# First experts' down product: the last 48 hidden channels in both partition halves, each half making 128 output channels in a bank of its own

## What is computed

```
h = silu(einsum('td,eid->eti', xt, W1)) * einsum('td,eid->eti', xt, W3)
expert_out = einsum('eti,edi->etd', h, W2)
y = einsum('etd,te->td', expert_out, combine)
z = silu(xt @ Ws1.T) * (xt @ Ws3.T) @ Ws2.T
```

## Time and profile before

| | us |
|---|---|
| median of 3 runs (1195.98 to 1196.88) | 1196.71 |
| the profiled execution | 1198.59 |
| span of its trace | 1196.8 |
| PE busy in the span | 1089.0 (91%) |
| DVE, ACT, POOL busy | 495.3, 503.4, 440.0 |

### The profile page before, as it was taken

How to read it: one execution, slowest core, us unless ns; L and a number is a source line. 1 busy time by engine, 2 the same in 40 slices (tenths; PEclk the granted TensorE clock), 3 DMA queues, 4 the chain that set the end, 5 groups by cost and what they waited for, 6 DMA issues and landing times. The chain is left out here.

```text
span 1196.8 us, 29018 instructions
## 1 busy us (share of the span) xinstructions
PE 1089.0 (91%) x10258; PEld 840.3 (70%) x10259; DVE 495.3 (41%) x1340; ACT 503.4 (42%) x1306; POOL 440.0 (37%) x563
## 2 busy tenths in 40 slices
PE   8889989988798689999988999998679999999998
PEld 4466666765465347777756777776579899899997
DVE  2365656555560013323325666766443800000423
ACT  2445554444432123333324666575334333333333
POOL 2122031311348852777644666332514100200434
PEclk9999999999998669999998999998789999999999
DMA  6199477120373334565546111000157655555673
GB/s 201 45 322 362 145 253 250 37 87 32 156 227 124 121 112 131 150 192 149 144 135 257 37 37 48 27 19 3 54 193 230 191 162 186 174 178 175 194 241 105
DMA packets 119340, 176.09 MB, mean 147 GB/s; under 512 B 17441, under 2 KB 96913, under 8 KB 117777
## 3 DMA queue, kind: packets, MB, share of 16 engines
q1 hardware_dynamic: 94992, 136.08, 35.4%
q0 software_dynamic: 9696, 26.75, 6.9%
q10 hardware_dynamic: 14544, 11.75, 3.0%
HBM read 105.07 MB, written 68.16 MB: 145 GB/s over the span
## 5 line engine op out<-in xcount | busy, mean ns | idle before, releaser
L3137 PE MATMUL bank<-w,m_HT 128*128 x624 | 141.0, 379 | 0.0
L2975 ACT ACTIVATE m_HT<-bank,m_b 128x128 f32<-128x128 f32 x312 | 88.8, 369 | 88.9 <-PE bank L3123 72.9
L3137 PEld LDWEIGHTS bank<-w,m_HT 128*128 128x128 f32 x624 | 115.7, 190 | 14.1
L1820 PE MATMUL bank<-m_W,m_XGT 128*128 x316 | 114.5, 487 | 10.8 <-issue 8.5
L1434 POOL DMA_INDIRECT GA<-ys,r_pos x64 | 64.7, 1010 | 64.7 <-DVE m_US L1764 46.5
L1677 ACT ACTIVATE m_XGT<-bank 128x256 f32<-128x256 f32 x79 | 30.3, 383 | 133.5 <-DVE m_US L1764 82.3
L1756 DVE TENSOR_TENSOR m_H<-bank,m_SG 128x176 f32<-128x176 f32 x79 | 26.9, 341 | 139.9 <-ACT m_SG L1681 108.0
L1820 PEld LDWEIGHTS bank<-m_W,m_XGT 128*128 128x128 f32 x316 | 57.0, 201 | 32.3 <-issue 16.4
L3123 PE MATMUL bank<-m_XGT,m_w1a 128*128 128x128 f32 x640 | 77.2, 279 | 2.3 <-issue 2.0
L2939 POOL DMA_INDIRECT m_GA<-ys,r_pos x32 | 31.4, 980 | 129.0 <-SPq L2890 120.0
L3123 PEld LDWEIGHTS bank<-m_XGT,m_w1a 128*128 128x128 f32 x640 | 75.0, 195 | 2.9 <-issue 2.3
(11 more groups left out here) (472 smaller groups left out, 2302.8 us busy)
## 6 DMA issues: line engine op xcount, KB each, us to landing
m_w1a<-in_m_w SPq DMA_DIRECT2D x20, 1024.0 KB
m_w<-in_m_w SPq DMA_DIRECT2D x19, 1024.0 KB
xs<-zeros SPq DMA_DIRECT2D x1, 10112.0 KB, 34.4
ys<-zeros SPq DMA_DIRECT2D x1, 10112.0 KB, 34.4
ys<-m_US ACTq DMA_DIRECT2D x79, 128.0 KB
m_GS<-xs SPq DMA_DIRECT2D x72, 128.0 KB
w<-in_m_w SPq DMA_DIRECT2D x8, 1024.0 KB, 10.6
xs<-zeros SPq DMA_DIRECT2D x1, 6400.0 KB, 23.4
```

The source lines that it names most:

```text
L1820: last = nc.tensor.matmul(BU[b % 2][:, 0:IW], XGT[:, b % 2, m * P:(m + 1) * P], W13[:, m, bass.ds(e, 1), :], start=m == 0, stop=m == KC - 1)
L2975: last = nc.scalar.activation(HT[:, b % 2, at, :], BU[i][:, c * P:(c + 1) * P], ACT.Gelu, bias=b1[:, b % WB, at:at + 1])
L3137: last = nc.tensor.matmul(BY[b % 2][:, 0:DIM], HT[:, b % 2, c, :], w2[:, bass.ds(e, 1), c, :], start=c == 0, stop=c == CH - 1)
```

## The change

The down product of a tile is cut into two halves of 128 output channels, and each half has a bank: `BY[0]` for the channels 0 to 127, `BY[1]` for 128 to 255, in every tile. The chunk of 128 hidden channels makes two matmuls of 128 columns (all 128 rows of the array). The rest of 48 is copied by ACT to partitions 0 to 47 and to 64 to 111 of `HT`. Then the first half's rest is multiplied from partitions 0 to 63 with `W2B`, and the second half's from partitions 64 to 127 with `odd[b]`: four buffers in the upper half of `W2B`, which SP fills per tile from DRAM (48 partitions of 512 bytes) with `load_odd`. Since both banks are used by every tile, the down product of tile j now waits until DVE has copied tile j - 1 out (`y_used`, counted one higher everywhere). DVE copies in two halves. Two small edits on POOL replace a semaphore by its step counter.

```diff
+        HALF = P // 2
+        odd = [W2B[HALF:P, b // 2, b % 2 * P:(b % 2 + 1) * P] for b in range(4)]
...
                     sp.dma_start(XG[:, b, :].unsqueeze(1), slots[:, bass.ds(s, 1), :]).then_inc(ld_x[b], 16)
+                    sp.wait_ge(ld_odd, 16 * j - 64)
+                    load_odd(j - 4, b)
+
+                def load_odd(j, b):
+                    e = sp.value_load(r.texp[0:1, bass.ds(j, 1)], min_val=0, max_val=E0 - 1)
+                    sp.dma_start(odd[b][0:KI].unsqueeze(1), io["w2"][P:I0, bass.ds(e, 1), P:DIM]).then_inc(ld_odd, 16)
...
+                sp.wait_ge(ld_w, 80)
+                for j in range(FIRST - 4):
+                    if j:
+                        sp.wait_ge(ld_odd, 16 * j)
+                    load_odd(j, j)
                 load(FIRST, FIRST % 4, FIRST)
...
+                for j in range(NT - 4, NT):
+                    sp.wait_ge(ld_odd, 16 * j)
+                    sp.wait_ge(y_full, j - 3)
+                    load_odd(j, j % 4)
...
                     nc.scalar.activation(HT[:, b % 2, 0, :], BH[b % 2][:, 0:P], ACT.Copy)
-                    nc.scalar.activation(HT[0:KI, b % 2, 1, :], BH[b % 2][0:KI, P:2 * P], ACT.Copy).then_inc(ht_used, 1)
+                    for lo in (0, HALF):
+                        last = nc.scalar.activation(HT[lo:lo + KI, b % 2, 1, :], BH[b % 2][0:KI, P:2 * P], ACT.Copy)
+                    last.then_inc(ht_used, 1)
...
-                    nc.vector.tensor_copy(Y[:, b % 2, :], BY[b % 2][:, 0:DIM]).then_inc(y_used, 1)
+                    for half in range(2):
+                        last = nc.vector.tensor_copy(Y[:, b % 2, half * P:(half + 1) * P], BY[half][:, 0:P])
+                    last.then_inc(y_used, 1)
...
-                    if not follows(ahead, 2):
-                        pe.wait_ge(y_used, j - 1)
+                    pe.wait_ge(y_used, j + 1)
                     pe.wait_ge(ht_used, j + 1)
-                    nc.tensor.matmul(BY[b % 2][:, 0:DIM], HT[:, b % 2, 0, :], W2A[:, bass.ds(e, 1), :],
-                                     start=True, stop=False)
-                    nc.tensor.matmul(BY[b % 2][:, 0:DIM], HT[:, b % 2, 1, :], W2B[:, bass.ds(e, 1), :],
-                                     start=False, stop=True).then_inc(y_full, 1)
+                    for half in range(2):
+                        nc.tensor.matmul(BY[half][:, 0:P], HT[:, b % 2, 0, :],
+                                         W2A[:, bass.ds(e, 1), half * P:(half + 1) * P], start=True, stop=False)
+                    pe.wait_ge(ld_odd, 16 * j + 16)
+                    nc.tensor.matmul(BY[0][:, 0:P], HT[0:HALF, b % 2, 1, :], W2B[0:HALF, bass.ds(e, 1), 0:P],
+                                     start=False, stop=True)
+                    nc.tensor.matmul(BY[1][:, 0:P], HT[HALF:P, b % 2, 1, :], odd[b], start=False, stop=True).then_inc(y_full, 1)
```

More of the change, by code:

```diff
@@ L1529, in moe0 @@
         z_full, z_used = sem("z_full"), sem("z_used")
-        sent, in_place, z_added = [sem(f"sent{b}") for b in range(2)], sem("in_place"), sem("z_added")
+        sent, in_place, ld_odd = [sem(f"sent{b}") for b in range(2)], sem("in_place"), sem("ld_odd")
+        HALF = P // 2
+        odd = [W2B[HALF:P, b // 2, b % 2 * P:(b % 2 + 1) * P] for b in range(4)]
         slots, rows_out = (x.rearrange("(s p) d -> p s d", p=P) for x in (fx.xs, fx.ys))
@@ L1609, in add_shared @@
                     pool.wait_ge(z_used, t // 2 + 1)
-                    nc.gpsimd.tensor_tensor(part, part, Z[:, t, half * P:(half + 1) * P], ALU.add).then_inc(z_added, 1)
+                    return nc.gpsimd.tensor_tensor(part, part, Z[:, t, half * P:(half + 1) * P], ALU.add)
                 for t in range(TILES):
@@ L1621, in _ @@
                 landed(TILES - 1)
+                own = fx.pool_steps
                 for half in range(2):
-                    add_shared(TILES - 1, half)
-                pool.wait_ge(z_added, 2 * TILES)
-                own = fx.pool_steps
+                    last = add_shared(TILES - 1, half)
+                own(pool, last)
                 def may_fetch(t):
-                    pool.wait_ge(y_used, pool.value_load(r.ready[0:1, t:t + 1], min_val=3, max_val=NT + 2))
+                    pool.wait_ge(y_used, pool.value_load(r.ready[0:1, t:t + 1], min_val=4, max_val=NT + 3))
                     pool.sem_inc(due, 1)
@@ L1685, in turned_product @@
                     nc.scalar.activation(HT[:, b % 2, 0, :], BH[b % 2][:, 0:P], ACT.Copy)
-                    nc.scalar.activation(HT[0:KI, b % 2, 1, :], BH[b % 2][0:KI, P:2 * P], ACT.Copy).then_inc(ht_used, 1)
+                    for lo in (0, HALF):
+                        last = nc.scalar.activation(HT[lo:lo + KI, b % 2, 1, :], BH[b % 2][0:KI, P:2 * P], ACT.Copy)
+                    last.then_inc(ht_used, 1)
                 def store(j, b):
                     s = act.value_load(r.tslot[0:1, bass.ds(j, 1)], min_val=0, max_val=NT - 1)
-                    act.wait_ge(y_used, j + 1)
+                    act.wait_ge(y_used, j + 2)
                     act.dma_start(rows_out[:, bass.ds(s, 1), :], Y[:, b % 2, :].unsqueeze(1)).then_inc(stored[b % 2], 16)
@@ L1749, in _ @@
                                ((POOL_GATES, POOL_GATES + 1), (POOL_GATES + 2,)))
-                r.ready_on_dve(nc, dve, fx.ident[:], BU[0], BU[1], 2, gated,
+                r.ready_on_dve(nc, dve, fx.ident[:], BU[0], BU[1], 3, gated,
                                ((POOL_GATES + 3,), (POOL_GATES + 4,)))
@@ L1763, in step @@
                     dve.wait_ge(stored[b % 2], 8 * (j + (2 - b % 2)))
-                    nc.vector.tensor_copy(Y[:, b % 2, :], BY[b % 2][:, 0:DIM]).then_inc(y_used, 1)
+                    for half in range(2):
+                        last = nc.vector.tensor_copy(Y[:, b % 2, half * P:(half + 1) * P], BY[half][:, 0:P])
+                    last.then_inc(y_used, 1)
+                dve.sem_inc(y_used, 1)
                 product(0, 0)
```

## The result

The kernel after takes 1232.72 us (median of 4, 1229.84 to 1233.63) where the kernel before takes 1196.8 (median of 4: the three executions of the table above and one of 1202.01): ratio 1.0281, 95% interval 1.0255 to 1.0307, 36 us slower. The span of its trace is 1230.4 us.

A forecast was written before the change was run, and what follows sets the result against it. PE was taken to bound the steady steps, late handovers the scatter stretch. PE's steps 10.1, SP's chain 3.3, scatter stretch 3.5 and tail 0.8 sum to 17.7 us over 1196.7: 1214 us, range 1204 to 1230.

The forecast's parts named there:

- Full-array part: Down product on PE, chunk of 128 hidden channels: four passes of 128 columns cost 0.448 us instead of 0.434, +0.014.
- paired part: Down product's rest of 48 on PE: row halves run side by side, 0.22 us instead of 0.434, plus changes of form.
- round trip: PE's way into the half-row form and out again around the down product: 0.33 to 0.34 us a step.
- SP's chain: SP's odd loads per tile: serial loop of landing, table read and issue, 2.63 us; +3.3 us after slack of 6.3.
- need rounds: SP, first 32 tiles: every fourth round has a third table read and the `in_place` wait, 0.87 us each, 7.0 us.
- SP sets the pace: Rival: landing takes 2.1 us or more and PE stops each step at `ld_odd`; 1222 to 1235 us, chance 0.20.
- Scatter stretch: 390 to 436 us, while POOL scatters: waiting for the previous tile's copy closes a loop, 10.6 us a step; +3.5 us.
- Tail: End of the tile loop: the last two down products both wait for two copies, +0.8 us.

The follow-up runs named there:

- before_half_rows: The kernel before with the last 48 channels' two passes on 64 array rows alone, same bank, nothing paired; 1167.81 us beside 1142.74, ratio 1.0229.
- two_in_flight: The kernel after with odd transfers alternating between two semaphores, so SP waits for the last landing but one; 1163.76 us, ratio 1.0169 to the kernel before.
- two_in_flight_early: The kernel after with two semaphores for odd transfers and the second layer's weights requested at about 320 us; 1159.84 us, ratio 1.0129 to the kernel before.
- before_cut: The kernel before with the down product's four passes of 256 columns cut into eight of 128, same bank; 1206.16 us beside 1194.27, ratio 1.0095.
- full_rows_two_banks_b: The kernel after without form change, odd transfers and ACT's second copy, last 48 channels over all 128 rows; fourth chip, 1217.41 us beside 1199.53, ratio 1.0156.
- after_again: The kernel after, unchanged, run on the second chip; 1172.85 us, ratio 1.0253 to the kernel before.

## Why the prediction was wrong in size

The direction, and most terms of the sum, held. One was several times too small, and it put the time outside the range of 1204 to 1230 us; a small one was missing.

- **Full-array part and paired part: right.** 0.142 us a step was forecast, 2.64 - 2.49 = 0.15 measured. The round trip of 0.34 us read from rows 4 and 5 is what before_half_rows shows by itself, and the halves pair.
- **SP's chain: the failed step.** "7.0 + 2.6 - 6.3 = +3.3 us" came out at 15.5 us on the second chip and 13.8 on the fourth (medians). By the distances from tile 10 to 75 it is 14.0 and 11.8 there, and on the first some 22.8 - 65 x 0.19 = 10.5. Two inputs were off. The landing was taken as 1.9 us throughout; idle it is 1.6, but in traffic up to 3.0, and waiting for one at a time costs 9.1 us (two_in_flight). And `weights()` was costed by the 2.9 us in which it holds the queue, not by the bytes in front of the next landing: 253 to 267 GB/s from 548 to 554 us, odd weights that PE could use 4.0 us after their issue instead of 1.9, and the granted clock of 0.50 behind the stop. The stop is 7.9 us in that trace, 2.6 were forecast; with two semaphores in place, taking it away gave 3.9 us more. SP's own rounds, which the sum charged with 7.0 us against a slack of 6.3, were not the trouble: the need rounds cost 1.0 each and not 0.87, and two_in_flight_early still loses nothing by them. The prediction saw the steepness ("+14 us more" from 2.15 us on) and put it into the rival *SP sets the pace*, 1222 to 1235 us, with a chance of 0.20. That rival's time came true; its shape did in part, since PE stopped for SP in single steps and once for long, and not in each.
- **Missing: the queue of PE.** The prediction counted passes by their duration alone. Shorter passes leave the queue less lead for its table reads; before_cut shows it, and the kernel after loses at most 0.04 us a step by it, 0.5 to 2.4 us in 65 steps. Also, `ld_odd` is waited for by register work of the queue (the order after shows `REGISTER_ALU [waits m0_ld_odd]`), so a late landing should also delay the table read behind it. I read this from the order and have not measured it alone.
- **Scatter stretch: the loop as forecast, its price not settled.** The loop was forecast at 10.6 us a step and ran at 10.9. From 390 to 436 us four down products begin, as forecast; before it were five, where the prediction read 5.8 steps from the number of passes. The price of +3.5 us, with 0.3 for the form in the two steps from tile 8 to 10, stands against 4.9 us on the first chip and 3.8 on the fourth. That full_rows_two_banks_b loses nothing while in the loop forbids calling this more than agreement of one or two traces; it may be luck.
- **Tail: small.** 0.8 forecast; the distance from tile 75 to 78 grows by 1.0 us, and the last product itself by 0.7.
- **Not in the sum: 3 us ahead of the first tile.** Tile 0 starts 3.0 us later on the first chip and 4.1 on the fourth, but 0.3 earlier on the second. By 334 us, before any edited instruction, PE of the two kernels already stands 2.9, 1.7 and -3.2 us apart. Most of it is thus variation between executions. Counted from POOL's first scatter, tile 0 comes 0.6, 0.9 and 0.9 us later in the kernel after; that part may be of the edits.

The sum of the distances on the first chip: 3.0 + 4.9 + 8.6 + 7.7 + 6.5 + 1.0, and 0.7 for the last product, is 32.4 of the 33.6 us between the spans.

## What to carry to other kernels

A transfer added to each step of a loop is a chain of its own. Cost it at the landing time in the traffic where it runs, keep more than one in flight (9.1 us here), and ask which bulk transfer will ever stand in front of it. Splitting the contraction into row halves pays only if the pair saves more than the round trip into the form, here 0.34 us for each visit against 0.2 saved. Halving the length of passes in a loop with register addresses takes lead from the engine's queue: before_cut's step is 2.60 to 2.65 us instead of 2.49, though its passes add up to only 0.03 us more.

## What the runs showed of the hardware

The late handovers of the scatter stretch went with the chip and not with the kernel: all eight traces from the second chip are without them (25.4 to 29.0 us from tile 0 to 10), all traces of the other three have them (53.9 to 64.8). The same kernel before, in the window of the same place on the fourth and on the second chip:

```profile
390.00:436.00 46.00, 27.36 (x61) 15.03 (x61) 4.26 (x11) 6.17 (x23) 37.38 (x48) 0.59 0.36 123
```

```profile
390.00:436.00 46.00, 46.00 (x220) 34.05 (x219) 14.12 (x37) 17.22 (x72) 37.66 (x47) 1.00 0.60 194
```

POOL is as busy in both. On the second chip PE runs at full pace and 0.60 of the DMA engines' time is used instead of 0.36; the whole kernel takes 1142.8 us there instead of 1199.6, and 35 of these us lie between tile 0 and tile 10. The copies are not late there (in after_again they end 1.0 to 1.4 us ahead of the next down product), so that the loop does not close. What in the chip makes the difference no run here shows. The change costs 30 us on the second chip, 33 on the fourth and 36 on the first.
